# Loads of a fused four-layer kernel moved ahead into preceding blocks and layer norms

## The reference

```python
# layer 2, attention: causal self attention, then 16 heads of width 8 over the context
a = _mha(inputs, inputs, inputs, Wk1, Wv1, Wq1, Wo1, bo1, masked=True)
a = _layernorm(inputs + a, g1, b1)
c = _mha(context_seq, context_seq, a, Wk2, Wv2, Wq2, Wo2, bo2, masked=False)
c = _layernorm(c + c, g2, b2)
f = relu(c @ Wf + bf)
return _layernorm(c + f, g3, b3)

# layer 2, feed-forward: weights quantised to -1, 0, 1 by their mean, tokens to 8 bits
h = bit_linear(x, w1)            # 128 -> 512
h = depthwise_conv1d(h, conv_w, conv_b); h = silu(h)
return bit_linear(h, w2)         # 512 -> 128

# layer 3, attention: one head, keys, values, queries and output layer-normed
qk = einsum('bqd,bkd->bqk', ln1(query), ln2(key)) / inv_scale_factor
return ln4(einsum('bqk,bkd->bqd', softmax(qk), ln3(value)))

# layer 3, feed-forward: 8 routed experts (2 for each token) and a shared one, 128 -> 256 -> 128
```

## Time and profile before

| | |
|---|---|
| median of three runs | 3592.65 us (3586.34 to 3593.73) |
| the profiled execution | 3594.13 us, its span 3592.4 us |
| busy: PE, DVE, POOL, ACT | 86%, 64%, 52%, 49% of the span |
| mean granted TensorE clock | 0.909 of full speed |
| DMA | 367.71 MB moved, mean 102 GB/s |

### The profile page before, as it was taken

The page is one execution under the profiler, slowest core; times in us unless marked ns, Lnnn a source line. Parts: engine busy times, 40 slices in busy tenths (PEclk is TensorE's granted clock), DMA queues, the critical chain, the costliest instruction groups (busy, mean ns, idle before and its releaser), DMA issues. The chain is left out here.

```text
span 3592.4 us, 75092 instructions
## 1 busy us (share of the span) xinstructions
PE 3089.1 (86%) x30284; PEld 2146.4 (60%) x30284; DVE 2302.8 (64%) x4272; ACT 1744.5 (49%) x2862; POOL 1864.5 (52%) x1046
## 2 busy tenths in 40 slices
PE   5977995999999999999959996799999983419959
PEld 3654544777777777777738775355555542216634
DVE  3546554777777777777634444699899865633445
ACT  2534332666665666656624543366666651104535
POOL 0003544777777777777632110488788770005316
PEclk9988996999999999999979997699999995559979
DMA  5740005766767666766514663343333310054500
GB/s 96 143 123 1 1 1 108 144 139 132 146 129 139 139 132 138 141 135 141 96 41 179 241 238 148 89 102 94 91 101 91 95 37 6 0 86 87 103 29 11
DMA packets 607381, 367.71 MB, mean 102 GB/s; under 512 B 462933, under 2 KB 566626, under 8 KB 606786
## 3 DMA queue, kind: packets, MB, share of 16 engines
q1 hardware_dynamic: 607042, 362.96, 43.7%
HBM read 174.41 MB, written 75.24 MB: 69 GB/s over the span
## 5 line engine op out<-in xcount | busy, mean ns | idle before, releaser
L1674 POOL TENSOR_TENSOR L_plo<-L_p,L_phi 128x1500 bf16<-128x1500 f32 x224 | 659.1, 2942 | 291.2 <-DVE L_phi L1750 289.8
L1631 ACT COPY L_ptlo<-L_lt 128x1536 bf16<-128x1536 bf16 x224 | 322.1, 1438 | 406.3 <-PE L_lt L1571 406.3
L2020 ACT ACTIVATE L2b_p<-L2b_score 125x448 f32<-125x448 f32 x768 | 378.7, 541 | 276.8 <-PE L2b_score L1933 274.2
L1585 PE MATMUL L_acc<-L_chi,L_pthi 125*128 125x128 bf16 x2688 | 462.1, 219 | 0.0
L1587 PE MATMUL L_acc<-L_chi,L_ptlo 125*128 125x128 bf16 x2688 | 461.4, 219 | 0.0
L1586 PE MATMUL L_acc<-L_clo,L_pthi 125*128 125x128 bf16 x2688 | 461.2, 219 | 0.0
L1739 DVE TENSOR_SCALAR_CACHE_REDUCE L_p<-L_score,L_cols 128x1500 f32<-128x1500 f32 x224 | 395.3, 1765 | 83.0 <-PE L_score L1563 82.8
L1750 DVE CAST L_phi<-L_p 128x1500 bf16<-128x1500 f32 x224 | 297.5, 1328 | 164.1 <-ACT L_p L1625 163.2
L1625 ACT ACTIVATE L_p<-L_p,L_least 128x1500 f32<-128x1500 f32 x224 | 346.5, 1547 | 67.4 <-DVE L_p L1739 63.3
L2063 POOL TENSOR_TENSOR L2b_psum<-L2b_p 125x896 f32<-125x896 f32 x128 | 266.9, 2085 | 134.6 <-ACT L2b_p L2020 132.2
L2091 DVE TENSOR_REDUCE L2b_max<-L2b_m 112x1 f32<-112x1000 f32 x256 | 300.4, 1194 | 26.6 <-PE L2b_m L1914 18.8
(11 more groups left out here) (632 smaller groups left out, 6917.5 us busy)
## 6 DMA issues: line engine op xcount, KB each, us to landing
L2b_kst<-L_keys SPq DMA_DIRECT2D x96, 375.0 KB, 5.6
L_ct<-L_ct SPq DMA_DIRECT2D x32, 768.0 KB, 5.7
L2a_ct<-L_ct SPq DMA_DIRECT2D x32, 768.0 KB, 14.3
L_ctx<-dram_ctx SPq DMA_DIRECT2D x32, 750.0 KB
L_keys<-L2a_kout SPq DMA_DIRECT2D x32, 750.0 KB, 7.6
L_values<-L2a_vout SPq DMA_DIRECT2D x32, 750.0 KB
L2b_vin<-L_values SPq DMA_DIRECT2D x32, 750.0 KB
L0x_ctx<-dram_ctx SPq DMA_DIRECT2D x32, 672.0 KB
```

What stands on the lines that cost most here:

```text
L1585: pe.matmul(acc, w_hi[0:KP, t, :], v_hi[0:KP, t, :], start=(t == 0), stop=False)
L1631: act.copy(pt_lo[g % 2][:, :, :], lt_ps[:, 0:KT * 128].rearrange("p (t q) -> p t q", t=KT)).then_inc(lo_read, 1)
L1674: pool.tensor_tensor(p_lo[g % 2][:, :, 0:KP], probs[g % RP][:, :].rearrange("q (t k) -> q t k", t=KT), p_hi[g % 2][:, :, 0:KP], ALU.subtra ...
L2020: act.activation(probs[t % RP][:, half * 2 * GW:(half + 1) * 2 * GW], score_ps[half][0:KP, 0:2 * GW], ACT.Exp).then_inc(exp_done, 1)
```

## The change

It takes the loads out of blocks of their own.

- `early_tensors` and `Early`: 39 weights and columns of layers 2 and 3 get places in SBUF for the whole program and are loaded by SP inside the expert block of layer 0 (`on_sync`). Engines wait for all of them once, with one semaphore that is never cleared.
- The causal mask is built in the first block of layer 0.
- `layernorm` takes `on_sync` and `on_pool`: work for SP, and for GpSimd behind its second power. The first three context pairs are issued in the norm ahead of the self attention. The waits for the stored keys and values and the first two key stacks go into the norm behind it; GpSimd fills the rows of ones of stacks 1 and 2 there, VectorE that of stack 0 in the next block behind the constants, all as 3000 f32 words in place of 6000 bf16.
- The two quantising blocks become one that treats both matrices.
- The ring of layer 3's attention (20 DMAs) and its two memsets go into `bit_ffn`; its reciprocal goes into the block behind the norm. The expert weights are issued behind the last ring load of layer 3's attention.

```diff
 def layernorm(..., double=False, twice=False,
+              on_sync=None, on_pool=None):
                     pool.tensor_tensor(rstd[:, a:b], var[:, a:b], c["half_neg"][:, a:b], ALU.pow).then_inc(rstd_ready, 1)
+                if on_pool is not None:
+                    pool.wait_ge(rstd_ready, 2 * k + 2)
+                    on_pool(pool)
+            if on_sync is not None:
+                @block.sync
+                def _(sp):
+                    on_sync(sp)
...
+    def load(self, sp):                              # class Early
+        for dst, src in self.pairs:
+            sp.dma_start(dst, src).then_inc(self.sem, 16)
...
 layer0_ffn: split_experts(..., 
+            "on_sync": c["early"].load})
...
 paired_head:
-                for n in range(R, P):
+                for n in range(mode["begun"], P):
                     wait(sp, av_done, n - R + 1)
                     ring.load(sp, n)
+                if "load_next" in mode:
+                    mode["load_next"](sp)
...
 narrow_heads_attention:
-                sp.wait_ge(consts_ready, 1)
-                for dst_, src_ in ((wq[:, :, :], "wq"), (wo[:, :], "wo"), (own[:, :], "own")):
-                    sp.dma_start(dst_, i[f"{name}_{src_}"]).then_inc(w_loaded, 16)
-                for n in range(B):
+                for n in range(2, B):
                     wait(sp, av_done, KT * (n - RK + 1))
-                    load(n)
+                    stacks["load"](sp, n)
...
-                for k in range(RK):
-                    dve.memset(k_stack[k][96:R, :, :], 1.0)
                 for k in range(2):
                     dve.memset(negmax[k][:, :], 0.0)
                 dve.memset(v_one[:, :], 1.0)
                 dve.tensor_copy(delta[96:R, :], c["ident"][96:R, 96:R]).then_inc(consts_ready, 1)
                 dve.wait_ge(consts_ready, 1)
-                dve.wait_ge(w_loaded, 16 * 3)
+                stacks["one_rows"](dve, 0).then_inc(ones_ready, 1)
...
+    def one_rows(eng, k):
+        return eng.memset(k_stack[k][96:R, :, :].rearrange("r g n -> r (g n)").bitcast(F32), pair_of_ones)
...
 self_attention:
-                for k in range(2):
-                    sp.wait_ge(k_stored[k], 16 * (B // 2))
-                    sp.wait_ge(v_stored[k], 16 * (B // 2))
...
 layer2_attention:
+            layernorm(nc, c, "L2x_ln", c["xT"], c["hT"], 1e-5, on_sync=first_ct)
...
+            def first_stacks(sp):
+                for k in range(2):
+                    sp.wait_ge(stored["k"][k], 16 * (B // 2))
+                    sp.wait_ge(stored["v"][k], 16 * (B // 2))
+                for b in range(2):
+                    stacks["load"](sp, b)
+            def one_rows(pool):
+                for k in range(1, stacks["RK"]):
+                    stacks["one_rows"](pool, k).then_inc(rows_made, 1)
+                    pool.wait_ge(rows_made, k)
+            layernorm(nc, c, "L2x_ln1", cT, c["hT"], 1e-6, col["g1"][:, :], col["b1"][:, :], on_sync=first_stacks,
+                      on_pool=one_rows)
...
 quantise_weights (one block for both matrices):
+                for k in range(2):
+                    m = dve.tensor_reduce(total[:, k:k + 1], w[k][:, :], AX.X, ALU.add, apply_absolute_value=True)
+                m.then_inc(total_ready, 1)
+                dve.wait_ge(sum_done, 1)
+                st.link(dve.tensor_scalar(level[:, :], ps[:, 0:2], 1.0 / COUNT, 1e-5, ALU.mult, ALU.max))
+                st.link(dve.reciprocal(inv[:, :], level[:, :]))
+                dve.tensor_scalar(w[0][:, :], w[0][:, :], inv[:, 0:1], MAGIC, ALU.mult, ALU.add)
+                st.link(dve.tensor_scalar(w[1][:, :], w[1][:, :], inv[:, 1:2], MAGIC, ALU.mult, ALU.add))
+                for k in range(2):
+                    m = dve.tensor_scalar(w[k][:, :], w[k][:, :], MAGIC, 1.0, ALU.subtract, ALU.min)
+                st.link(m)
+                for k in range(2):
+                    dve.tensor_scalar(out[k][:, :], w[k][:, :], -1.0, None, ALU.max)
...
 run_layers:
+            layer2_ffn(nc, c, ring_loads, query_zeros)
+            clear_used(nc)
+            layer3_attention(nc, c, i, held, expert_loads)
+            clear_used(nc)
+        layer3_ffn(nc, c, raw3, w_loaded3)
```

More of the change, by code:

```diff
@@ L426, in _ @@
                         act.copy(gate_sb[g % 2][:, :], g_ps[g % 2][:, 0:CH]).then_inc(gate_ready, 1)
+            if spec.get("on_sync") is not None:
+                @block.sync
+                def _(sp):
+                    spec["on_sync"](sp)
             @block.gpsimd
@@ L518, in top2, with router @@
             cur = rest
-def router(nc, c, name, src, spec, gatesT, sel, loaded):
+def router(nc, c, name, src, spec, gatesT, sel, loaded, on_sync=None):
     E, deep = spec["E"], spec.get("gw1") is not None
@@ L788, in __init__ @@
         self.ctx = [space.sb(f"{name}_ctx{r}", [KP, 2, KT, D + 1]) for r in range(R)]
-        self.loaded = [space.sem(f"{name}_ctx_loaded{r}") for r in range(R)]
+        self.loaded = [nc.alloc_semaphore(f"{name}_ctx_loaded{r}") for r in range(R)]
     def load(self, sp, n):
@@ L1080, in _, with run_steps @@
                 normalise(P - 1)
-def run_steps(nc, name, loads, steps):
+def run_steps(nc, name, steps):
     with Space(nc) as sp_:
-        loaded, done = sp_.sem(f"{name}_loaded"), sp_.sem(f"{name}_done")
+        done = sp_.sem(f"{name}_done")
         def run(eng, who):
@@ L1091, in run @@
                 if w == who:
-                    if loads:
-                        eng.wait_ge(loaded, 16 * len(loads))
                     if n:
@@ L1098, in run_steps @@
         with nc.Block() as block:
-            @block.sync
-            def _(sp):
-                for dst, src in loads:
-                    sp.dma_start(dst, src).then_inc(loaded, 16)
-                if loads:
-                    sp.wait_ge(loaded, 16 * len(loads))
             @block.tensor
@@ L1155, in _ @@
                 pool.memset(shift[:, :], 0.0)
+                causal_mask(pool, causal_made, c["causal"], late)
             @block.tensor
@@ L1237, in layer0_attention @@
         paired_head(nc, c, "L0x", ring, q_pad, o_all, {
-            "kind": "standard", "shift": shift, "factor": factor, "query": query, "shifts": shifts,
+            "kind": "standard", "begun": ring.R, "shift": shift, "factor": factor, "query": query, "shifts": shifts,
             "read_query": read_query, "read_shifts": read_shifts})
@@ L1323, in layer3_attention @@
         paired_head(nc, c, "L3x", ring, q_pad, o_all, {
-            "kind": "normed", "shift": shift, "query": query, "shifts": shifts, "read_query": read_query,
+            "kind": "normed", "begun": ring.R, "load_next": load_experts_next, "shift": shift, "query": query, "shifts": shifts, "read_query": read_query,
             "read_shifts": read_shifts})
@@ L1798, in narrow_heads_attention @@
     MAXU = 3 * P // 2
-    RK, RP = 3, 6
+    RK, RP = stacks["RK"], 6
+    k_stack, v_in, k_loaded, v_loaded = [stacks[k] for k in ("k_stack", "v_in", "k_loaded", "v_loaded")]
     SUMS = [(0, 1, 2), (3, 4, 5), (6, 7, 8), (9, 10)]
@@ L2154, in self_attention @@
     with Space(nc) as sp_:
[L2155 to L2156 removed]
+        wq, wk, wv, wo = [c[f"{name}_w{k}"] for k in "qkvo"]
+        own, cw = c[f"{name}_own"], c[f"{name}_cw"]
         q_all, k_all = sp_.sb(f"{name}_qall", [128, T]), sp_.sb(f"{name}_kall", [128, T])
@@ L2595, in layer2_ffn, with _ @@
-def layer2_ffn(nc, c, i):
+            @block.tensor
+            def _(pe):
+                pe.wait_ge(total_ready, 1)
+                pe.matmul(ps[:, 0:2], c["ones"][:, :], total[:, :], start=True, stop=True).then_inc(sum_done, 1)
+            @block.vector
+            def _(dve):
+                st = Steps(dve, step)
+                for k in range(2):
[11 more added lines that the diff above has]
+                    dve.tensor_scalar(out[k][:, :], w[k][:, :], -1.0, None, ALU.max)
@@ L2827, in run_layers, with ring_loads, query_zeros, expert_loads @@
     clear_used(nc)
-    layer2_ffn(nc, c, i)
-    clear_used(nc)
-    layer3_attention(nc, c, i)
-    clear_used(nc)
-    layer3_ffn(nc, c, i)
-    clear_used(nc)
+    with Space(nc) as experts_space:
+        dram3 = {"w1": i["L3f_w1"], "w2": i["L3f_w2"]}
+        raw3 = expert_tensors(experts_space, "L3f", dram3, 9, 2)
+        w_loaded3 = [nc.alloc_semaphore(f"L3f_w_loaded{e}") for e in range(9)]
+        with Space(nc) as ring_space:
+            held = {"ring": Ring(nc, ring_space, "L3x", i["ctx"], 5),
+                    "q_pad": ring_space.sb("L3x_qpad", [128, B, 64]),
+                    "shift": ring_space.sb("L3x_shift", [128, B // 2])}
+            def ring_loads(sp):
+                for n in range(held["ring"].R):
+                    held["ring"].load(sp, n)
+            def query_zeros(pool):
+                pool.memset(held["q_pad"][:, :, S:64], 0.0)
+                pool.memset(held["shift"][:, :], 0.0)
+            def expert_loads(sp):
+                for e in range(9):
```

(4 more changed lines are left out.)

271 lines of the change are left out of this document (139 added, 132 removed).

## The result

The changed kernel takes 3486.55 us (median of 4 runs, 3485.49 to 3489.05) against 3593.19 us (3586.34 to 3593.92). The ratio is 0.9708, with a 95% interval of 0.9694 to 0.9721: faster. The profiled execution took 3485.49 us (span 3483.8), 108.6 less than the 3594.13 of before; the prediction's sum was 105, its time 3487.5.

A forecast was written before the change was run, and what follows sets the result against it. The span was taken as stages, one engine full in each, plus seams between them where DMA engines are full. Six seam gains sum to 105 us, from the median 3592.65 to 3487.5; range 3477 to 3501.

The forecast's parts named there:

- Seam 1: Into layer 2's first attention: TensorE's idle time before the projections falls from 14.18 to 0.94 us, gain 13.2 us.
- Seam 2: Into layer 2's second attention: stores' wait 7.1, norm to query product 20.15, stack waits 2.25; gain 29.5 us.
- that is what is late next: Norm behind the self attention: GpSimd's two memsets and their waits end 1.7 us past the norm's end.
- Seam 3: Product with wf: TensorE's idle 2.93 us falls to 0.94 and 0.24, gain 1.75 us.
- Seam 4: Quantised weights: norm end to the next block's first operation falls from 13.95 to 6.75 us, gain 7.2 us.
- Seam 5: Into layer 3's attention: norm starts 41.1 us earlier, 0.4 for a warmer norm, 0.3 back for the reciprocal; gain 41.2 us.
- The warmer norm: Layer 3's norms: 14 transposes take 2.12 us behind a short gap, not 3.22; about 0.4 us reaches the end.
- Seam 6: Into layer 3's experts: idle falls from 14.19 to 2.41 us, 0.4 more for the warmer norm; gain 12.2 us.
- Case A: Small terms miss together: full-clock start at seams gives 3483, dearer memsets 3494; forecast with these ends 0.82, gain beyond 0.04.
- Case B: Quantised layer: ring loads delay its loop's instruction fetch, a few us up to 36.4, giving 3494 to 3524; chance 0.10.
- Case C: Layer 2's second attention: clock falls, at share 0.83 the result is 3605, slower than before; chance 0.02.
- Case D: Seams stay because a moved load is still waited for; with other losses of 7 to 40 us, chance 0.02.

The follow-up runs named there:

- The two experiments on that norm: Changed kernel with SP loading stacks 0 and 1 behind their own stores only, 3488.9 us; the same with GpSimd's first fill ahead of its powers, 3484.0 us.
- the bf16 run: Changed kernel with the rows of ones filled as 6000 bf16 elements in place of 3000 f32 words: 3489.5 us.
- two chains of 3.2 us in the experiment: Changed kernel with the two matrices quantised in two blocks one after the other, from weights loaded early: 3485.9 us.
- the experiment splits it: Changed kernel with layer 3's 20 ring loads and two zero fills back in a block of their own ahead of the norm: 3518.5 us.
- the starved stage: Layer 0's attention with a ring of three pairs, not four, and layer 1's loads moved, on the kernel with layer 0's loads moved: 3538.0 us.
- filler: 14 more transposes on TensorE in each layer norm: 3482.1 us on the changed kernel, 3419.3 us on the one with layer 1's loads moved and four pairs.

## Why the prediction was right

**Seam 1 (13.2).** 13.25: norm to projections 24.44 us before (1850.45 to 1874.89), 11.19 after. The clock there gained nothing, as taken. The 39 early loads cost nothing: layer 0's experts take 271.1 us from norm to norm, 271.5 before. The mask costs nothing either: it is done at 3.4 us, and SP's loads hold that first block open until 36.2.

**Seam 2 (29.5).** 30.2. The stores' wait was 7.04 (7.1 in the sum). Norm to query product gave 20.5, of it 0.5 because that norm's transposes happened to run at full clock (1.72 us against 3.22); the sum had 20.15. The stack waits gave 2.6 against 2.25. GpSimd's fills took 2.6 us each, near the lower bound and not the 3.0 taken. Wrong was "that is what is late next": the fills were through at 2210.2, 0.9 us past VectorE, and SP's issue at 2210.9. The last store, issued until 2196.8, took 10.5 us and landed 9.2 us behind the norm's start. The working had it land 7 us behind (2222.5, where the new norm would start at 2215.53 in the old kernel's time), and the text said that two microseconds more would let SP hold the block open. They did. That the overrun was 1.6 us where 1.7 was foreseen is luck: the fills were 0.8 us cheaper and SP was late, and the two errors cancel. The two experiments on that norm show SP first and the fills behind it, 1.8 us in all.

The Trainium skill (VectorE: DVE Perf Modes, section Zero memsets can be issued as uint32) has a memset cost by the element whatever its type; the bf16 run agrees, on both engines. Its one cycle for each element would be an estimated 3.1 us for 3000 at its clock of 0.96 GHz. VectorE's row says 2.56, but the row is not the whole cost, as the first two fills of the kernel before show beside the third in the earlier trace rows:

```profile
2235.83 5.06 DVE L2128 MEMSET L2b_kst<- 4x6000 bf16 x1 [1.57 <-issue]
2242.09 5.06 DVE L2128 MEMSET L2b_kst<- 4x6000 bf16 x1 [1.20 <-issue]
```

They start 6.26 us apart, 1.04 ns for each element, with nothing between them to wait for; and the idle time ahead of a fill grows with it, 0.68 us ahead of 3000 elements after and 1.31 ahead of 6000 in the bf16 run. So a fill costs VectorE what the page says, 6.3 us for 6000 and some 3.1 for 3000, and the 5.06/6000 = 0.84 ns of the prediction was read off too short a row.

**Seam 3 (1.75).** The idle time fell by exactly 1.75. To the next norm's start it is 1.9: wf's product was 0.5 quicker, the norm ahead of it 0.45 slower, both by clock.

**Seam 4 (7.2).** 8.1. The term for the fused block was too large: 4.8 us and not 6.0, since the second matrix's passes follow the first's at 0.34 to 0.40 us and not 0.45, and its links are 0.03 us apart (two chains of 3.2 us in the experiment), where those of the old chain of 3.95 us, each of them with a wait for the loads as well, were 0.10 apart (3003.37 to 3003.47).

**Seam 5 (41.2).** 41.3 to the norm's start, and the experiment splits it. The warmer norm (0.4) did not come, here or in seam 6: 3.22 us for the 14 transposes after 1.6 and 2.2 us of idleness as after 43. What ran ahead of both was itself at half clock: the quantised layer at 0.50, and the later transposes of the norm before seam 6 at 2.39 us for ten. But that is no proof of the cause. The prediction had its 2.12 us from one norm of the kernel before, with ten transposes at 2.40 us ahead of it as well, and the same norm takes 3.22 us after, behind the same gap of 2.41. What sets the clock there stays open. The block of the reciprocal cost 0.5 in place of 0.3.

**Seam 6 (12.2).** 12.0.

**Sum.** The seams gave 106.3 us (13.25 + 30.2 + 1.9 + 8.1 + 41.3 - 0.5 + 12.0) against 105. The other 2.3 us of the profiled pair are not in the seams and within the spread: the first norm of layer 2 already starts 2.15 us earlier, and all that the change adds ahead of it are the early loads and the mask.

**The rivals.** Case A's full-clock start did not come, and the memsets were cheaper and not dearer. Case B: turns of 39.97 us against 39.83. The Trainium skill (Runtime: NRT & Kernel Launch, section Instruction fetch mechanics) would have a branch outside what the engine holds wait for a fetch; whether this loop branches so no row tells, but with the DMA engines full under its first turn nothing of the kind shows beyond 0.3 us. Case C: 596.9 of 600 us at a clock of 1.00. (Its 3605 for a share of 0.83 was summed wrongly: 596/0.83 is 122 us more, which gives 3610.) Case D: no moved load is waited for; the 11 waits of GpSimd for the ring in layer 3 (74.9 us in all, 73.3 before) are for the later pairs.

## What to carry to other kernels

What a load costs a seam depends on what the block waits for. Where nothing in the block needs the data, it costs SP's issue: 0.45 us for a small load, and 1.7 to 1.8 us for each of the ring's 20 with the DMA engines full; four of the same loads took 4.4 us in the starved stage, where the engines had room. Where the block waits for the data, it costs the whole way to landing as well: 6.5 us for the two weights of seam 4. Put such loads in the queue of a block whose SP only waits, but ask first which engine would then be last in that block, and whether the loads it is moved past still come in time. Room in SBUF for early loads must not be taken from a ring that needs it: one buffer less cost 112 us here, more than the six seams had given.

## What was not expected of the hardware

- GpSimd fills faster than VectorE: 2.60 to 2.62 us for 3000 f32 and 5.12 for 6000 bf16, against some 3.1 and 6.26 us from one fill's start to the next on VectorE. VectorE's own rows, 2.56 and 5.06, are too short. A GpSimd fill beside VectorE's statistics did not slow them (1.69 us for eight, 1.68 without it).
- Starving costs twice: with 88.4 us of waits spread over layer 0's attention the granted clock was 0.79, with none it was 1.00, and the same products kept TensorE busy 27 us longer, which is about the 24 us that the stage lost on top of the waits.
- The clock just behind a seam is not the same from one kernel to the next: of the twelve kernels the 14 transposes of the norm behind the self attention took 1.72 us in three, 2.28 and 3.00 in one each, and 3.22 in seven. The router's first four passes took 1.74 us in five of the ten kernels without filler, with the same work ahead of them.
